# Cross-attention with a layer norm: earlier, differently cut loads of wo, and another order of the last deviations

## The reference

```python
Q = (query @ w_q.T).reshape(B, S, NUM_HEADS, D_K).transpose(0, 2, 1, 3)
K = (key @ w_k.T).reshape(B, -1, NUM_HEADS, D_K).transpose(0, 2, 1, 3)
V = (value @ w_v.T).reshape(B, -1, NUM_HEADS, D_K).transpose(0, 2, 1, 3)
scores = jnp.einsum('bhqd,bhkd->bhqk', Q, K) / np.sqrt(D_K)
attn = jax.nn.softmax(scores, axis=-1)
ctx = jnp.einsum('bhqk,bhkd->bhqd', attn, V).transpose(0, 2, 1, 3).reshape(B, S, D_MODEL)
x = ctx @ w_o.T + b_o + query
mu = jnp.mean(x, axis=-1, keepdims=True)
var = jnp.mean(jnp.square(x - mu), axis=-1, keepdims=True)
return (x - mu) * jax.lax.rsqrt(var + LN_EPS) * ln_gamma + ln_beta
```

## Time and profile before

| what | value |
|---|---|
| median of 3 runs | 559.01 us (558.89 to 560.57) |
| the profiled execution's own time | 557.26 us |
| its span (first to last instruction or transfer) | 555.5 us |
| PE busy | 532.4 us (96%) |
| DVE busy | 465.2 us (84%) |
| POOL busy | 424.2 us (76%) |
| ACT busy | 393.6 us (71%) |
| bytes moved by DMA | 63.23 MB, mean 114 GB/s |

### The profile page before, as it was taken

How to read it: one execution, slowest core, us unless ns; L and a number is a source line. 1 busy time by engine, 2 the same in 40 slices (tenths; PEclk the granted TensorE clock), 3 DMA queues, 4 the chain that set the end, 5 groups by cost and what they waited for, 6 DMA issues and landing times.

```text
span 555.5 us, 12699 instructions
## 1 busy us (share of the span) xinstructions
PE 532.4 (96%) x4522; PEld 363.1 (65%) x4522; DVE 465.2 (84%) x874; ACT 393.6 (71%) x733; POOL 424.2 (76%) x391
## 2 busy tenths in 40 slices
PE   8988899999999999999999999999999999998991
PEld 6755566766676666666676667666676667665561
DVE  7877668888888888988889888988888888988785
ACT  7636767777777777777777777777777777766662
POOL 1714678888888888888888888888888888776665
PEclk9999999999999999999999999999999999999997
DMA  8434552443344334443343334343343432222122
GB/s 312 143 86 122 153 167 70 131 130 95 95 131 131 102 93 125 131 122 88 110 133 108 112 105 127 107 128 100 118 114 106 133 102 84 86 67 69 48 76 95
DMA packets 74111, 63.23 MB, mean 114 GB/s; under 512 B 46528, under 2 KB 46528, under 8 KB 74048
## 3 DMA queue, kind: packets, MB, share of 16 engines
q1 hardware_dynamic: 74048, 62.42, 37.0%
HBM read 39.58 MB, written 16.78 MB: 101 GB/s over the span
## 4 chain that ended last, share of the span: by engine, by line
PE 84%; DVE 5%; SPq 3%; DMA 3%; POOL 2%; issue 2%; ACT 1%; POOLq 0%; DVEq 0%; ACTq 0%
PE ps_q L410 45%; PE ps_o L416 12%; PE ps_c L372 10%; PE ps_s L345 7%; PE ps_s L355 3%; PE ps_q L283 2%; PE ps_s L283 2%; PE ps_o L283 2%; SPq L217 2%; DMA wo_raw<-in_woT 2%; DMA max_rows<-max_turned 1%; DVE half_max L703 1%; POOL y L879 1%; PE ps_c L290 1%; POOL y L877 1%
## 5 line engine op out<-in xcount | busy, mean ns | idle before, releaser
L410 PE MATMUL ps_q<-x_hi,wq_lo 64*128 64x512 f32 x448 | 185.8, 415 | 1.2 <-DVE values L668 1.1
L416 PE MATMUL ps_o<-wo_hi,c_lo 64*128 64x512 f32 x448 | 186.3, 416 | 0.0
L416 PE MATMUL ps_o<-wo_hi,c_hi 64*128 64x512 f32 x448 | 175.4, 392 | 0.0
L410 PE MATMUL ps_q<-x_hi,wq_hi 64*128 64x512 f32 x448 | 175.3, 391 | 0.0
L410 PE MATMUL ps_q<-x_lo,wq_hi 64*128 64x512 f32 x448 | 175.1, 391 | 0.0
L416 PE MATMUL ps_o<-wo_lo,c_hi 64*128 64x512 f32 x448 | 174.7, 390 | 0.0
L410 PEld LDWEIGHTS ps_q<-x_hi,wq_lo 64*128 64x128 f32 x448 | 82.5, 184 | 74.6 <-DVE z L747 44.4
L877 POOL TENSOR_TENSOR y<-y,gamma_row 128x512 f32<-128x512 f32 x60 | 77.8, 1296 | 58.4 <-ACT y L562 58.4
L849 POOL TENSOR_TENSOR x_lo<-xT_raw,x_hi 128x512 fp32r<-128x512 f32 x60 | 77.4, 1290 | 27.3 <-ACT x_hi L497 23.3
L855 POOL TENSOR_TENSOR c_lo<-c_raw,c_hi 128x512 fp32r<-128x512 f32 x64 | 82.9, 1295 | 16.7 <-ACT c_hi L497 16.7
L410 PEld LDWEIGHTS ps_q<-x_hi,wq_hi 64*128 64x128 f32 x448 | 82.6, 184 | 16.2
(11 more groups left out here) (104 smaller groups left out, 1113.6 us busy)
## 6 DMA issues: line engine op xcount, KB each, us to landing
xT_raw<-in_xT SPq DMA_DIRECT2D x64, 256.0 KB, 3.2
x_raw<-in_x SPq DMA_DIRECT2D x64, 256.0 KB, 2.8
out<-y SPq DMA_DIRECT2D x64, 256.0 KB, 2.4
max_rows<-max_turned SPq DMA_DIRECT2D x256, 16.0 KB
ctx_raw<-in_ctxT SPq DMA_DIRECT2D x4, 256.0 KB, 4.7
wk_raw<-in_wkT SPq DMA_DIRECT2D x4, 256.0 KB, 4.8
wq_raw<-in_wqT SPq DMA_DIRECT2D x4, 256.0 KB, 5.8
wv_raw<-in_wvT SPq DMA_DIRECT2D x4, 256.0 KB, 6.6
```

What stands on the lines that cost most here:

```text
L410: return nc.tensor.matmul(ps_q[:, 0, :], w[l][half, k, dims], x_[r][half, qc % 2, k, :], start=(half is lower and k == 0 and step == 0), s ...
L416: return nc.tensor.matmul(ps_o[:, 0, :], cx[l][half, k, tile], wo[r][half, k, :], start=(half is upper and k == 0 and step == 0), stop=(ha ...
```

## The change

Five things. (1) SP: wo goes out as four transfers of 32 partitions and all four blocks each, and they, the bias, gamma and beta rows and the x tiles 0 to 3 are issued before the wait for the keys, ahead of slot 0; the x tiles 4 to 7 follow one in each of slots 2 to 5. ACT waits once, in slot 3, for all of wo. (2) PE: in slots 1 to 3 `subtract_max(t - 1)` comes before `project_values`. (3) DVE: in slot 6 `odd_values` comes before `turn_max`. (4) DVE: slot 62 is written out, with `turn_max(61)` ahead of `divide(59)` and `statistics(54)`; and `finish(58)` comes before `statistics(59)`. (5) ACT: `invert_deviation(57)` and `(58)` come earlier, and for tiles 59, 60 and 61 ACT makes the shift itself, in two instructions on 128x1 (`shift_mean` on ACT), in place of POOL.

```diff
-            sp.wait_ge(keys_zeroed, 2)
-            sp.wait_ge(keys_lo_done, G)
...
+            for quadrant, head in enumerate((0, 2, 1, 3)):
+                sp.dma_start(wo_raw[DK * quadrant:DK * (quadrant + 1), :, :],
+                             woT.rearrange("(k h d) n -> h d k n", k=KT, h=4)[head, :, :, :]).then_inc(wo_loaded, 16)
+            sp.dma_start(bias_row[:, :], b_o.partition_broadcast(P)).then_inc(bias_loaded, 16)
+            for row, src in ((gamma_row, gamma), (beta_row, beta)):
+                sp.dma_start(row[:, :], src.partition_broadcast(P)).then_inc(gains_loaded, 16)
+            for i in range(4):
+                load_x(i)
+            sp.wait_ge(keys_zeroed, 2)
+            sp.wait_ge(keys_lo_done, G)
             for t in range(OUT_LAG):
                 fill_max_rows(t)
                 load_ahead(t)
-
-                if 1 <= t <= KT:
-
-                    for head in range(2):
-                        sp.dma_start(wo_raw[64 * head:64 * (head + 1), t - 1, :],
-                                     woT_v[t - 1, :, :].rearrange("(p h d) n -> h p d n", p=2, h=2)[head, :, :, :]
-                                     ).then_inc(wo_loaded[t - 1], 16)
-                if t == 1:
-                    sp.dma_start(bias_row[:, :], b_o.partition_broadcast(P)).then_inc(bias_loaded, 16)
                 if 2 <= t <= 5:
-                    load_x(2 * t - 4)
-                    load_x(2 * t - 3)
-                if t == 5:
-                    for row, src in ((gamma_row, gamma), (beta_row, beta)):
-                        sp.dma_start(row[:, :], src.partition_broadcast(P)).then_inc(gains_loaded, 16)
+                    load_x(t + 2)
                 next_keys(t)
@@ tensor
             for t in range(OUT_LAG):
                 score(t)
                 project_queries(t + 1)
+                if 1 <= t <= 3:
+                    subtract_max(t - 1)
...
-                if 1 <= t < OUT_LAG - 1:
+                if 3 < t < OUT_LAG - 1:
                     subtract_max(t - 1)
@@ scalar
+            def shift_mean(i):
+                c = i % 8
+                nc.scalar.activation(shift[:, c:c + 1], mean_var[:, c, 0:1], ACT.Identity, scale=-1.0
+                                     ).then_inc(mean_negated_done, 1)
+                act.wait_ge(mean_negated_done, by_scalar(i) - by_scalar(59) + 1)
+                act.wait_ge(rstd_done, i + 1)
+                nc.scalar.activation(shift[:, c:c + 1], shift[:, c:c + 1], ACT.Identity, scale=rstd[:, c:c + 1]
+                                     ).then_inc(shift_done, 1)
...
                 if 3 <= t < 3 + KT:
-                    split_hi(wo_hi, wo_raw, t - 3, wo_loaded, wo_hi_done, 32)
+                    if t == 3:
+                        act.wait_ge(wo_loaded, 16 * 4)
+                    to_hi(wo_hi[:, t - 3, :], wo_raw[:, t - 3, :]).then_inc(wo_hi_done, 1)
...
             invert_deviation(56)
+            invert_deviation(57)
             context_to_hi(62)
             normalise(56)
             log_sums(63)
             invert_sums(63)
-            invert_deviation(57)
+            invert_deviation(58)
             context_to_hi(63)
-            invert_deviation(58)
-            invert_deviation(59)
-            normalise(59)
-            invert_deviation(60)
-            normalise(60)
-            invert_deviation(61)
-            normalise(61)
+            for i in (59, 60, 61):
+                invert_deviation(i)
+                shift_mean(i)
+                normalise(i)
             invert_deviation(62)
             invert_deviation(63)
@@ vector
                 queries_to_lo(t + 1)
+                if t == OUT_LAG - 1:
+
+                    odd_values(t // 2)
                 turn_max(t)
-                if t % 2 == 0:
+                if t % 2 == 0 and t < OUT_LAG - 1:
                     odd_values(t // 2)
 
-            for t in range(OUT_LAG, SLOTS - 1):
+            for t in range(OUT_LAG, SLOTS - 2):
...
+            turn_scores(61)
+            half_maxima(61)
+            fold_halves(61)
+            turn_max(61)
+            divide(59)
+            statistics(54)
+            add_residual(55)
+            queries_to_lo(63)
             statistics(55)
...
             finish(57)
             divide(63)
+            finish(58)
             statistics(59)
-            finish(58)
             add_residual(60)
@@ gpsimd
             for i in (59, 60, 61):
-                shift_mean(i)
                 scale(i)
```

More of the change, by code:

```diff
@@ L121, in by_scalar @@
             return i - sum(d < i for d in BY_VECTOR)
-        ctx_loaded, wk_loaded, wv_loaded, wq_loaded, wo_loaded = (
-            [sem(f"{n}_loaded{k}") for k in range(KT)] for n in ("ctx", "wk", "wv", "wq", "wo"))
-        bias_loaded, gains_loaded = sem("bias_loaded"), sem("gains_loaded")
+        ctx_loaded, wk_loaded, wv_loaded, wq_loaded = (
+            [sem(f"{n}_loaded{k}") for k in range(KT)] for n in ("ctx", "wk", "wv", "wq"))
+        wo_loaded, bias_loaded, gains_loaded = sem("wo_loaded"), sem("bias_loaded"), sem("gains_loaded")
         xT_loaded = [sem(f"xT_loaded{k}") for k in range(KT)]
@@ L156, in cross_attention_kernel @@
         last_scaled_done, last_y_done = sem("last_scaled_done"), sem("last_y_done")
+        mean_negated_done = sem("mean_negated_done")
         def key_blocks(t, s, j):
@@ L497, in to_hi, with split_hi @@
                 return nc.scalar.activation(dst, src, ACT.Copy)
-            def split_hi(hi, raw, k, loaded, done, value=16):
-                act.wait_ge(loaded[k], value)
+            def split_hi(hi, raw, k, loaded, done):
+                act.wait_ge(loaded[k], 16)
                 to_hi(hi[:, k, :], raw[:, k, :]).then_inc(done, 1)
```

## The result

The changed kernel takes 555.27 us (median of 6 runs, 552.56 to 555.67) against 558.95 us before (6 runs, 557.97 to 560.57), ratio 0.9922 with an interval of 0.9898 to 0.9946. It is faster by 3.7 us where I had forecast 8.6, and it lies above the upper end of the range, 553.7.

The account below looks back on a forecast made before the run. PE was taken to bound the kernel (84% of the chain), so only its gaps and the end could give time: 4.6 us at the start plus 4.0 at the end, 8.6, from 559.01 to 550.4 us; range 548.5 to 553.7.

Parts of the forecast that it names:

- Part 1: Loads ahead of slot 0: eleven issues, 2.9 MB, take 7.2 us and are done at 27.7, barely touching max_rows(0).
- I take the fast end: Loads ahead of slot 0: transfers into 32 partitions assumed at 399 GB/s, between bounds of 44 and 399.
- Part 2: Slots 1 to 6: shorter waits of PE bring the first project_both from 73.44 to 68.8, a gain of 4.6 us.
- Part 3: Last slots: reordering and the shift on ACT make the last store go at 548.9 against 552.9, 4.0 us.
- 0.7 off the 1.44: finish(62) on DVE: its 1.44 us instruction gets some 0.7 shorter as DVE's 2.66 idle before it goes.
- The 0.7 for finish(57): Last slots: with invert_deviation(57) early, the wait for rstd(57) ahead of divide(63) goes, 0.7 us more.
- 0.6 for PE's wait: Last slots: PE's 1.56 wait at 513.86 goes with turn_max(61) earlier, but only 0.6 us of it is kept.
- z(60) waited for finish(58) anyway: Last slots: finish(58) first costs statistics(59) 1.7 us, but z(60) loses nothing by it.
- The shift on ACT: Tiles 59 to 61: normalise(61) comes at 542.6, rstd(62) at 543.9 instead of 548.05, and DVE's 2.66 idle goes.
- the prediction's own sign (over 437): Long loop: more than 437 us from project_both to score(62) would show the prediction wrong.
- The burst is late: Start: loads last past 28 us, max_rows(0) lands at 33 to 34, price 1 to 2.6 us; chance 0.17.
- the end gives half: Last slots: DVE and POOL on the same tiles hold the last store, half of 4.0, giving 552.4; chance 0.14.

Follow-up runs that it names:

- the narrow scale: Changed kernel with POOL's scale of tiles 59 to 61 working on 16 of 512 columns: 551.64 us, ratio 0.9881.
- the last experiment but one: Changed kernel with only wo ahead of slot 0 and finish(58) put back behind statistics(59): 550.65 us, ratio 0.9847.
- the end alone: Kernel before with only the change's DVE and ACT edits to the last slots: 555.25 us, ratio 0.9940.

## Why the prediction was right in its sign and wrong in its size

- **Part 1, the burst of loads, is the step that failed first.** "I take the fast end", 399 GB/s for all 2.9 MB. wo moved at 206 to 222 GB/s (370 in whole blocks), and the broadcast rows at 155 where they could be seen apart (with wo in whole blocks). PE's wait in slot 1 was 2.1, not 0.6: 1.5 us of the 3.1 that are missing at the start. The row that I leaned on, the key fills' 2.4 us to landing, is a latency of 32 KB and says nothing of a rate. The rule that I cited and left out of the sum, the Trainium skill, SBUF — State Buffer, section on the DMA port swizzle, gives half rate for 32 partitions; the traces agree (206 to 222 against 370), and by it the forecast would have been up to 2 us nearer.
- **A term was missing: the clock behind the wait.** The sum had none. In the changed kernel it is 1.5 us in slots 1 and 2, the other half of the missing 3.1. The profile of before gave no hint, since it kept 1.00 behind a wait of 2.00 and one of 1.56; before, profiled again, did not.
- **Part 2 otherwise held.** Clean slots took 6.9 to 7.0, slot 6 took 7.3 (64.71 to 72.03), the exponential's 1.2 went, max_rows waits nowhere in slots 4 and 5, odd_values gave its 0.5 and ACT's one wait cost nothing. With the burst made short (only wo ahead) the start took 47.29 against the forecast 47.0, with a wait of 0.8 in slot 1 against 0.6.
- **Part 3: the contention had the wrong sign, the second step that failed.** I took 0.7 off the 1.44 of the earlier trace rows since DVE's idle time would go. With both engines back to back DVE lost more, not less: 1.52 + 1.56 + 1.43 + 0.75 is 5.3 where I had 3.3. With that gone (the narrow scale) the end took 38.1 against my 37.9; that it is so close is in part luck, since z(60) was 0.4 late and the four instructions took 3.0 and not 3.3. The Trainium skill, SBUF — State Buffer, section "SBUF: two separate sides", says that a DVE instruction with two SBUF inputs and a GpSimd instruction that reads SBUF exclude each other for a whole instruction; the traces agree: DVE's 1.56 at 545.19 overlaps POOL's 1.59 from 544.62, and is 0.75 without it.
- **The 0.7 for finish(57) did not come, for the same reason.** The timeline of DVE, first before, then after:

```profile
532.16 1.01 DVE L760 SCALAR_TENSOR_TENSOR y<-z,mean_var,gamma_row 128x512 f32<-128x512 f32 x1
534.29 0.75 DVE L765 SCALAR_TENSOR_TENSOR y<-y,rstd,beta_row 128x512 f32<-128x512 f32 x1 [1.12 <-ACT rstd L555]
```

```profile
530.95 1.41 DVE L769 SCALAR_TENSOR_TENSOR y<-z,mean_var,gamma_row 128x512 f32<-128x512 f32 x1
532.46 1.60 DVE L774 SCALAR_TENSOR_TENSOR y<-y,rstd,beta_row 128x512 f32<-128x512 f32 x1
```

The wait of 1.12 for rstd(57) went, and the two instructions, now close together beside POOL's, took 1.25 more. z(59) was 1.05 earlier after score(62) than before, where I had kept 0.6 for PE's wait; divide(63) only 0.8, z(60) 0.85 and not 1.2 (28.52 against 29.37).

- **finish(58) ahead of statistics(59) was not free.** "z(60) waited for finish(58) anyway" is true (z(60) is as early with either order), but tile 59's mean was on the way of ACT and POOL: 0.7 us by the last experiment but one.
- **The shift on ACT was right**: rstd(62) at 544.16 (forecast 543.9), normalise(59) to normalise(61) from 539.75 to 543.13, and 2.6 us when it is taken back.
- **The loop** took 1.2 more, and by the prediction's own sign (over 437) that was to show it wrong. From score(7) to score(62), 55 slots, about 0.5 of it is a usual slot of mostly 7.84 where the one before has 7.82; the other 0.7 is single longer slots (8.02, 7.95, 8.30 and 8.54, against 8.00, 8.36 and 7.92). But executions with this very loop differ as much: project_both to score(62) is 436.5 with the narrow scale, 437.0 with the shift on POOL and 438.9 with finish(58) put back. So it is no part of the change that I could name. What sets it stays open.
- **The rivals and the range.** "The burst is late" (0.17) and "the end gives half" (0.14) both happened, and the first with the clock's price on top. I had built the range from one rival at a time; the two together with my own prices, 2.6 and 2.0, would have reached 555.0, and the clock's 1.5 beyond the result.

The account between the medians: 8.6, less 3.1 at the start, less 1.2 of loop, less about 1.9 at the end (4.0 to 2.1), is 2.4, the difference of the two profiles. The other 1.3 us would be the clock behind max_rows(61), which the first profile of before didn't pay. That most executions of before pay it is not shown: of those without a profile only the mean clock is on record, 0.986 to 0.994 where the first profile has 0.995.

## What to carry to other kernels

Price a transfer by a row with the same partitions and the same cut, and where there is none, carry the slower rate into the sum or into the range: a full DMA share says that the engines are occupied, not that bytes move. A load issued early is free only if what the bound engine asks for next isn't behind it; here, the four loads of wo early and the other seven later was worth 3.2 us more than all eleven early. When engines that read the same memory are both made to run back to back, add their collisions instead of taking them off, and when rivals concern different places, add them up for the range.

## What was not expected of the hardware

- PE's clock fell to its lower level behind idle times of 1.67 to 2.19 us in slot 1 and of 1.62, 1.65 and 2.18 elsewhere, and not behind 1.56 and 2.00 in another execution of the same kernel, nor behind 1.89 in slot 4 of the end alone. It cost 1.4 to 1.6 us in slot 1 and at the end, and 0.1 in slot 4, where the next wait took it up. Eight useless products in the gap prevented it.
- Three rows of 2 KB, each broadcast to 128 partitions, moved 155 GB/s at a share of 0.84 (24 to 26 us with wo in whole blocks).
- The old cut also held up the queue that issues it: ahead of slot 0 its eight transfers took 13.66 us of SP, the four of the new cut 1.86.
- In halves, POOL's 128x512 of 1.3 us became 1.43 by itself and 1.73 to 1.85 with DVE at its two-input instructions in between.
- score(0) starts between 21.1 and 22.5 us by execution, so starts have to be compared by their distance from it.
